# Graph attention over 32 batches: the last batch turned wholly on TensorE, with its order written out

## The reference

```python
h = jnp.maximum(_layernorm(x, axis=-1), 0.0)
q = _heads(h @ Wq + bq)
k = _heads(h @ Wk + bk)
v = _heads(h @ Wv + bv)
scores = jnp.einsum('bhqd,bhkd->bhqk', q, k) / np.sqrt(HEAD_SIZE)
bias = jnp.where(graph_mask, 0.0, NEG)[:, None]
probs = jax.nn.softmax(scores + bias, axis=-1)
ctx = jnp.einsum('bhqk,bhkd->bhqd', probs, v)
x = x + (ctx.reshape(...) @ Wf + bf)
```

## Time and profile before

| | us |
|---|---|
| median of 3 runs (676.17 to 678.21) | 677.98 |
| the profiled execution's own time | 679.02 |
| span of its trace | 677.0 |
| busy in it: PE / DVE / ACT / POOL | 628.2 / 513.2 / 506.7 / 423.5 |

### The profile page before, as it was taken

How to read it: one execution, slowest core, us unless ns; L and a number is a source line. 1 busy time by engine, 2 the same in 40 slices (tenths; PEclk the granted TensorE clock), 3 DMA queues, 4 the chain that set the end, 5 groups by cost and what they waited for, 6 DMA issues and landing times. The chain is left out here.

```text
span 677.0 us, 20551 instructions
## 1 busy us (share of the span) xinstructions
PE 628.2 (93%) x6644; PEld 510.3 (75%) x6644; DVE 513.2 (76%) x1548; ACT 506.7 (75%) x1164; POOL 423.5 (63%) x459
## 2 busy tenths in 40 slices
PE   7638899999899998999999999999999999999985
PEld 5426788888788886888778877788878888888863
DVE  5626787788788877788778887788878888887774
ACT  1435888888788886788878876788778888888872
POOL 1335666767666666776666667576666776676551
PEclk8878899999999999999999999999999999999999
DMA  7015678767787686667877676776878668767563
GB/s 241 20 34 112 127 149 159 154 149 127 160 154 160 150 162 121 150 145 158 159 145 159 153 146 120 154 160 152 159 141 155 146 141 160 160 137 134 127 136 94
DMA packets 207684, 95.89 MB, mean 142 GB/s; under 512 B 152817, under 2 KB 207602, under 8 KB 207602
## 3 DMA queue, kind: packets, MB, share of 16 engines
q1 hardware_dynamic: 207602, 94.69, 67.7%
HBM read 17.05 MB, written 12.58 MB: 44 GB/s over the span
## 5 line engine op out<-in xcount | busy, mean ns | idle before, releaser
L632 DVE CUSTOM_DVE_ANT_0 logits<-scores,mask,logit_unscale 128x256 f32<-128x256 f32 x384 | 170.6, 481 | 128.0 <-PE scores L916 124.6
L432 POOL TENSOR_TENSOR p_rows<-probs,p_rows 128x512 f16<-128x512 f32 x128 | 151.0, 1180 | 183.1 <-ACT p_rows L513 183.1
L503 ACT ACTIVATE probs<-logits,raised 128x256 f32<-128x256 f32 x384 | 174.2, 500 | 6.3
L856 PE MATMUL ring<-h_hi,w_hi 128*128 128x256 f16 x576 | 159.1, 276 | 2.6 <-DVE w_lo L723 2.6
L857 PE MATMUL ring<-h_lo,w_hi 128*128 128x256 f16 x576 | 158.8, 276 | 0.0
L858 PE MATMUL ring<-h_hi,w_lo 128*128 128x256 f16 x576 | 158.6, 275 | 0.0
L416 POOL TENSOR_TENSOR split<-qk,split 128x512 f16<-128x512 f32 x96 | 111.1, 1157 | 13.1 <-DVE split L656 13.1
L915 PE MATMUL scores<-heads 128*128 128x256 f16 x384 | 95.3, 275 | 23.0 <-DMA heads<-split 16.9
L499 ACT ACTIVATE raised<-least,p_raise 128x2 f32<-128x2 f32 x192 | 56.8, 296 | 68.4 <-DVE least L632 53.3
L525 ACT ACTIVATE qk<-ring,qk_bias_s,qkv_ratio 128x256 f32<-128x256 f32 x192 | 97.0, 555 | 9.4 <-PE ring L858 8.6
L943 PE MATMUL ctx<-v_hi,p_cols 128*128 128x65 f16 x768 | 89.5, 194 | 14.0 <-DMA p_cols<-p_rows 9.8
(11 more groups left out here) (90 smaller groups left out, 1427.2 us busy)
## 6 DMA issues: line engine op xcount, KB each, us to landing
heads<-split SPq DMA_DIRECT2D x192, 96.0 KB, 2.2
x_in<-in_x_dram SPq DMA_DIRECT2D x32, 384.0 KB, 3.4
heads<-split SPq DMA_DIRECT2D x192, 64.0 KB, 2.1
out_dram<-result SPq DMA_DIRECT2D x64, 192.0 KB, 2.1
adj_in<-in_adj_dram SPq DMA_DIRECT2D x32, 64.0 KB, 2.0
p_cols<-p_rows SPq DMA_TRANSPOSE x128, 3.1
w_raw<-in_L_gnn_Wq_dram SPq DMA_DIRECT2D x1, 576.0 KB, 4.3
w_raw<-in_L_gnn_Wk_dram SPq DMA_DIRECT2D x1, 576.0 KB, 6.3
```

The lines of the kernel that those rows point to most:

```text
L432: pool.tensor_tensor(p_rows[u][:, 1], probs[u % 3][:], p_rows[u][:, 0], ALU.subtract).then_inc(p_lo_ready, 1)
L503: act.activation(probs[u % 3][:, a], logits[u % 3][:, a], ACT.Exp, bias=raised[u % 3][:, a:a + 1], scale=-1.0).then_inc(probs_ready, 1)
L632: dve.tensor_tensor_reduce(out=logits[u % 3][:, a], in0=score_bank[u % 2][:, a * S:(a + 1) * S], in1=mask[b.parity][:, t], scale=logit_uns ...
L856: pe.matmul(out_ap, a_hi, m_hi, start=first, stop=False)
```

## The change

For batch 31 alone, and with everything up to the end of cycle 30 left as it was:

- All six units are turned on TensorE. They take turns in two banks, `pt_bank` for even units and `ring[2]` for odd ones. ACT reads the high half and DVE the low half out of the bank (`last_hi`, `last_lo`). POOL's `probs_lo` for units 1, 2, 4 and 5 and SP's four transposing DMAs of this batch fall away. The two DMA units of batch 30 that cycle 31 still has to handle stay.
- The context of batch 31's first query tile goes into `ring[3]`, that of its second into `ctx_bank`.
- PE, DVE, ACT, POOL and SP no longer run cycles 31, 32 and 33. Each has its list of steps written out. On PE `last_transpose(u)` comes two slots behind `scores(u)`.

The three helpers stand, in this order, on ScalarE, VectorE and TensorE.

```diff
+        def ctx_of(b, t):
+            bank = ring[3] if b.k == B - 1 and t == 0 else ctx_bank
+            return bank[:, 0:HEADS * V1].rearrange("p (h d) -> p h d", h=HEADS)
...
-            for k in range(FIRST_IN_LOOP + RING * TURNS, B + 2):
+            for k in range(FIRST_IN_LOOP + RING * TURNS, B - 1):
                 cycle(Batch(0, k))
+        LAST = Batch(0, B - 1)
+        last_pt = [pt_bank, ring[2]]
...
+            def last_hi(u):
+                act.wait_ge(pt_ready, nth_last(u))
+                act.activation(p_cols[u][:, 0].rearrange("p a s q -> p (a s q)"), last_pt[u % 2][:],
+                               ACT.Copy).then_inc(pt_hi_ready, 1)
...
+            exps(LAST, 1)
+            last_hi(0)
+            context_hi(LAST + -1, 0)
+            exps(LAST, 2)
+            last_hi(1)
+            exps(LAST, 3)
+            last_hi(2)
...
+            def last_lo(u):
+                dve.wait_ge(pt_hi_ready, nth_last(u))
+                dve.tensor_tensor(p_cols[u][:, 1].rearrange("p a s q -> p (a s q)"), last_pt[u % 2][:],
+                                  p_cols[u][:, 0].rearrange("p a s q -> p (a s q)"),
+                                  ALU.subtract).then_inc(pt_lo_ready, 1)
...
+            finish(LAST + -2, 1)
+            last_lo(0)
+            mask_and_max(LAST, 2)
+            context_lo(LAST + -1, 0)
+            last_lo(1)
+            mask_and_max(LAST, 3)
+            divide(LAST + -1, 1)
+            last_lo(2)
+            mask_and_max(LAST, 4)
...
+            def last_transpose(u):
+                if u == 1:
+                    pe.wait_ge(v_lo_ready, LAST.count(2, 2))
+                pe.wait_ge(pt_lo_ready, nth_last(u - 2) if u >= 2 else LAST.count(len(PE_UNITS), 0))
...
+            apply_probs(LAST, 3)
...
+            project_out(LAST + -1, 1)
+            last_transpose(5)
+            apply_probs(LAST, 4)
+            project_out(LAST, 0)
+            apply_probs(LAST, 5)
+            transpose_context(LAST, 1)
+            project_out(LAST, 1)
```

More of the change, by code:

```diff
@@ L155, in gnn_attention @@
         R_OUT = [ring[1], ring[3]]
-        ctx_ps = ctx_bank[:, 0:HEADS * V1].rearrange("p (h d) -> p h d", h=HEADS)
+        def ctx_of(b, t):
+            bank = ring[3] if b.k == B - 1 and t == 0 else ctx_bank
+            return bank[:, 0:HEADS * V1].rearrange("p (h d) -> p h d", h=HEADS)
         w_in = [sem(f"w_in{n}") for n in range(4)]
@@ L267, in cycles, with nth_last @@
                     cycle(Batch(i, FIRST_IN_LOOP + n))
-            for k in range(FIRST_IN_LOOP + RING * TURNS, B + 2):
+            for k in range(FIRST_IN_LOOP + RING * TURNS, B - 1):
                 cycle(Batch(0, k))
+        LAST = Batch(0, B - 1)
+        last_pt = [pt_bank, ring[2]]
+        def nth_last(u):
+            return (B - 1) * len(PE_UNITS) + u + 1
         def nth_dma(u):
@@ L279, in probs_read @@
         def probs_read(eng, b, u):
-            if u in PE_UNITS:
+            if b.k == B - 1:
+                eng.wait_ge(pt_ready, nth_last(u))
+            elif u in PE_UNITS:
                 wait(eng, pt_ready, b.count(len(PE_UNITS), nth_pe(u)))
@@ L386, in _ @@
             cycles(sp, cycle)
+            place_heads(LAST, 2)
+            transpose_probs(LAST + -1, 4)
+            store(LAST + -2, 0)
+            transpose_probs(LAST + -1, 5)
+            store(LAST + -2, 1)
+            for b in (LAST + -1, LAST):
+                for t in range(QT):
+                    store(b, t)
             for t in range(QT):
@@ L485, in _ @@
             cycles(pool, cycle)
+            probs_lo(LAST + -1, 5)
         @block.scalar
@@ L490, in exps @@
             def exps(b, u):
[L492 to L495, removed]
+                if u >= 3:
                     probs_read(act, b, u - 3)
+                elif (b + -1).exists():
+                    probs_read(act, b + -1, u + 3)
                 wait(act, logits_ready, b.count(2 * UNITS, 2 * u + 2))
@@ L608, in _ @@
             cycles(act, cycle)
+            def last_hi(u):
+                act.wait_ge(pt_ready, nth_last(u))
+                act.activation(p_cols[u][:, 0].rearrange("p a s q -> p (a s q)"), last_pt[u % 2][:],
+                               ACT.Copy).then_inc(pt_hi_ready, 1)
+            probs_hi(LAST + -1, 5)
+            exps(LAST, 0)
+            v_hi_part(LAST, 1)
+            exps(LAST, 1)
[5 more added lines that the diff above has]
+            last_hi(2)
+            exps(LAST, 4)
+            last_hi(3)
+            context_hi(LAST + -1, 1)
+            exps(LAST, 5)
+            last_hi(4)
+            context_hi(LAST, 0)
+            last_hi(5)
+            context_hi(LAST, 1)
         @block.vector
@@ L667, in divide @@
                 wait(dve, ctx_ready, b.count(UNITS, C * (t + 1)))
+                ctx_ps = ctx_of(b, t)
                 dve.reciprocal(inv_sum[t][:], ctx_ps[:, :, D]).then_inc(inv_ready, 1)
@@ L849, in _ @@
             cycles(dve, cycle)
+            def last_lo(u):
[3 more added lines that the diff above has]
+                                  ALU.subtract).then_inc(pt_lo_ready, 1)
+            mask_and_max(LAST, 0)
+            divide(LAST + -1, 0)
+            mask_and_max(LAST, 1)
+            v_lo_part(LAST, 1)
+            finish(LAST + -2, 1)
[7 more added lines that the diff above has]
+            mask_and_max(LAST, 4)
+            finish(LAST + -1, 0)
+            last_lo(3)
+            mask_and_max(LAST, 5)
+            divide(LAST, 0)
+            context_lo(LAST + -1, 1)
+            last_lo(4)
+            context_lo(LAST, 0)
+            finish(LAST + -1, 1)
+            last_lo(5)
+            divide(LAST, 1)
+            finish(LAST, 0)
+            context_lo(LAST, 1)
+            finish(LAST, 1)
         @block.tensor
@@ L929, in apply_probs @@
                 t, j = u // C, u % C
-                if u in PE_UNITS:
+                ctx_ps = ctx_of(b, t)
+                if b.k == B - 1:
+                    pe.wait_ge(pt_lo_ready, nth_last(u))
+                elif u in PE_UNITS:
                     wait(pe, pt_lo_ready, b.count(len(PE_UNITS), nth_pe(u)))
@@ L935, in apply_probs @@
                     wait(pe, v_lo_ready, b.count(2, 2))
-                if j == 0:
+                if u == 0 and b.k == B - 1:
+                    pe.wait_ge(result_ready, (b + -2).count(2, 2))
+                elif u == C and b.k == B - 1:
+                    pe.wait_ge(context_ready, b.count(2, 0))
+                elif j == 0:
                     wait(pe, context_ready, b.count(2, t))
@@ L1038, in _ @@
             cycles(pe, cycle)
+            def last_transpose(u):
+                if u == 1:
+                    pe.wait_ge(v_lo_ready, LAST.count(2, 2))
+                pe.wait_ge(pt_lo_ready, nth_last(u - 2) if u >= 2 else LAST.count(len(PE_UNITS), 0))
+                for a in range(2):
+                    pe.wait_ge(probs_ready, LAST.count(2 * UNITS, 2 * u + a + 1))
+                    for s in range(QT):
+                        o = (a * QT + s) * P
+                        mm = pe.transpose(last_pt[u % 2][:, o:o + P], probs[u % 3][:, a, s * P:(s + 1) * P], ident[:])
+                mm.then_inc(pt_ready, 1)
+            scores(LAST, 0)
+            apply_probs(LAST + -1, 2)
+            project_out(LAST + -2, 1)
+            scores(LAST, 1)
+            apply_probs(LAST + -1, 3)
+            last_transpose(0)
+            scores(LAST, 2)
+            transpose_context(LAST + -1, 0)
+            apply_probs(LAST + -1, 4)
+            last_transpose(1)
+            scores(LAST, 3)
+            apply_probs(LAST + -1, 5)
+            last_transpose(2)
+            apply_probs(LAST, 0)
+            scores(LAST, 4)
+            project_out(LAST + -1, 0)
+            last_transpose(3)
+            apply_probs(LAST, 1)
+            scores(LAST, 5)
+            apply_probs(LAST, 2)
+            transpose_context(LAST + -1, 1)
+            last_transpose(4)
+            apply_probs(LAST, 3)
+            transpose_context(LAST, 0)
+            project_out(LAST + -1, 1)
[5 more added lines that the diff above has]
+            project_out(LAST, 1)
 _INS = ['x', 'adj', 'L0_gnn_Wq', 'L0_gnn_bq', 'L0_gnn_Wk', 'L0_gnn_bk', 'L0_gnn_Wv', 'L0_gnn_bv',
```

## The result

| | before | changed |
|---|---|---|
| median (us) | 678.58 (10 runs, 676.17 to 682.12) | 682.04 (10 runs, 681.16 to 684.66) |
| ratio to before | | 1.0049, 95% interval 1.003 to 1.0069 |
| span of the profiled execution (us) | 677.0 | 679.6 |
| from the first logits of batch 31 to the span's end (us) | 27.05 | 31.12 |

The change makes the kernel slower by 0.49%, about 3.3 us. The forecast was 680.5 us and +0.38%. The last line of the table is the measure for all that follows: everything up to the end of cycle 30 is the same code in every kernel here, but its time differs from one execution to the next (the first logits of batch 31 stand at 649.95 us before, at 648.48 after, and between 645.96 and 651.58 in all the profiles here). I call this measure the end. The spans are given to 0.1 us, so an end is known to about 0.05 us, though it is written with two digits.

What follows compares the result with a forecast made beforehand. TensorE bounds the body, chains of waits between engines the end. Logits 4.27 us late, less 1.28 and 0.43 regained, give +2.56 us with rounding; from 677.98 the forecast is 680.5 us, range 678.8 to 682.4.

Steps and rivals of the forecast that it cites:

- What goes: Last batch, unit 5: the 5.07 us DMA way goes; by TensorE 1.65 us, so applied 3.4 us earlier if nothing else were late.
- The closed round: Last batch, units 2 to 5: DVE and ScalarE pass one unit per 3.37 us, making logits(5) 4.27 us late.
- The sum to the end: From logits(5) to the span's end: 671.71 + 7.84 = 679.55 us of span, against 677.0, or +2.56 us.
- The time: Whole kernel: 680.5 us from a median of 677.98, or +0.38%.
- The bounds of what the trace didn't show: Last batch: simultaneous bank reads cost 0 to +0.7 us, hops 0.3 us either way; ends kept at -0.3 and +1.0 us.
- The clock: Rival: TensorE, idle more at 657 to 669 us, loses clock; at most +3.3 us, 683.8 us; chance 0.07.
- The first rival: Last batch: DVE and ScalarE keep ahead, removed DMAs come through; 676.7 us, outer bound 674.6; chance 0.07.
- The Trainium skill's rule of rotating banks: Turned probabilities' two banks: filling one while the other is read would make the last batch faster; no row showed bank waits.

Runs made afterwards that it cites:

- after_again: The changed kernel unaltered, profiled a second time: 678.22 us (one run), end 29.34 us.
- e1_logits_first: Changed kernel with VectorE's logits of units 3, 4 and 5 of the last batch put ahead of low halves 1, 2 and 3: 678.93 us, ratio 0.9991.
- e3_one_bank: Changed kernel with one bank instead of two for all six turned units: 681.51 us, ratio 1.0036.
- e5_fill_all: Changed kernel with 44 extra unread matmuls in TensorE's holes, 16 of them ahead of its last two waits: 680.77 us, ratio 1.0021.
- e4_searched: Changed kernel with the last batch's same steps in an order searched for the shortest end on TensorE, VectorE and ScalarE: 673.45 us, ratio 0.9919.
- e4_again: Changed kernel with the last batch's steps in the searched order on TensorE, VectorE and ScalarE, measured once more: 673.13 us, ratio 0.9912.
- e2_fill_matmul: Changed kernel with 28 extra unread matmuls in TensorE's holes between 655 and 666 us, the last two holes left open: 681.92 us, ratio 1.0044.
- e9_dma_searched: Kernel before, units 1, 2, 4 and 5 still turned by DMA and one context bank, last batch in an order searched likewise: 675.61 us, ratio 0.9961.

## Why the prediction was right, point by point

- **What goes.** Right. No transposing DMA is in the chain, and `apply_probs(31,5)` waits for TensorE's own work. From unit 5's last probability to that step it was 5.07 us before. In after_again, where the clock held, it is 3.6 us (forecast 3.78), and `project_out(30,1)` takes the 1.47 us of the earlier trace rows (664.85 to 666.32 in its timeline).
- **The closed round.** Right, and its size to 0.02 us: 3.37 forecast, 3.35 to 3.36 measured. Unit 5's logits are 15.70 - 11.46 = 4.24 us late, forecast 4.27. e1_logits_first shows the cause: with three steps of one list swapped the loss is gone.
- **The sum to the end.** Right where no fall of the clock lies on the chain: +2.29 us (after_again), +2.35 (e3_one_bank and e5_fill_all average 29.40), against +2.56. More than half of the difference is one term: `last_transpose(5)` took 0.44 us up to TensorE's next matmul in after_again, not 0.59. One step was left out by luck without harm. In TensorE's list `transpose_context(31,0)` stands ahead of `project_out(30,1)`, and the forecast let `context_lo` of batch 30 decide instead. The chain goes through the transposes (664.38, 0.55 us), and the projection starts 17.79 us behind the first logits, where the forecast had 17.86.
- **The time.** 682.04 us is 1.54 over the forecast of 680.5. Of this 0.60 is the base: the median of the kernel before was taken from three runs as 677.98 and is 678.58 over ten. The rest is taken up under the clock. That 682.04 still lies in the range (678.8 to 682.4) is in part luck, since no term of the range stood for a clock that falls on top of the forecast.
- **The bounds of what the trace didn't show.** In the round the high half is 0.57 to 0.58 us and the low half 0.69, as before. But ScalarE and VectorE don't read there at once: VectorE idles until the high half is done. They do in e4_searched, where the high half of unit 5 (662.25, 0.59 us) overlaps with the low half of unit 4 (662.45, 0.68 us) in the other bank for 0.39 us, and neither is longer by more than 0.02 us.
- **The clock.** Here the working was wrong in part. I had it as a rival with 7 in 100, to take the place of the forecast, at most +3.3 us. It doesn't take its place but comes on top, in some executions: 1.78 us in the first profile. I reasoned that a kernel whose clock held through a hole of 2.05 us would hold it through holes of 1.3 us. The rows show that it isn't the one longest hole: with holes of 0.94, 0.77 and 0.96 us one after another it fell in the first profile (in the third of them) and held in after_again, and in e3_one_bank it fell after one of 1.89. The size was wrong too. The 1.56 came from the lengths of single matmuls in the earlier trace rows (0.42 against 0.27 us). In a chain their spacing counts, and in the same trace it is 0.21 us (19.78 to 19.99) against 0.11 (22.18 to 22.29), twice as long, as is the 0.32 against 0.16 in `project_out(30,1)`. So the bound for 5.9 us of work, were all of it spaced so, was +5.9 and not +3.3 us. The clock is the likely rest of the 3.3 us measured beyond the 2.3 of the order, but that is argued from profiles. How many executions have the fall isn't known: the mean granted clock of every run (0.975 on average over the ten of the changed kernel, against 0.977 in the profile with the fall and 0.980 in the one without) speaks for many of them. But the first slices of a run move this mean as well (e4_again's profile has 0.975 with no fall in the end), so no count follows.
- **The first rival** (the round isn't closed and the DMAs' time comes through) was wrong for this order. e1_logits_first makes its condition true for units 3 to 5: the end is 0.71 us shorter than before, where the rival had 1.3, and unit 5's logits are still 0.60 us late (12.06 against 11.46). The searched order goes beyond it: 676.7 us and at best 674.6 were the rival's numbers, and 673.1 to 673.5 came out. There the search also moved the scores forward, and unit 5's logits stand at 8.43 us.
- **The Trainium skill's rule of rotating banks** (Perfetto Trace Analysis, Matmuls) holds once the lists let it: the second bank is worth nothing in the changed kernel's order (29.40 without it, 29.34 with it) and 3.6 us in the searched one.

## What to carry to other kernels

When an order is written out, go round the waits once per unit: if engine A has step x(u-1) ahead of step y(u+1), and engine B has its part of x(u-1) behind its part of y(u), the two engines work one after the other, and each unit takes one turn of that round, whatever else is freed. Its length can be added up from a few rows of the old trace, and it came out here to two hundredths of a microsecond. While the round was closed, the faster way for a step (TensorE for the DMA) gave back 5.07 - 3.60 = 1.47 us of the 4.24 that the round cost, and the second buffer nothing. Once it was open, the second buffer was worth 3.6 us.

## What the hardware showed that I had not expected

- TensorE's granted clock at the end of one and the same program: 0.57 between 665 and 669 us in one execution, 1.00 all through the end in the next. In the kernel before, with a hole of 2.05 us, its one profile shows 1.00. The level was 0.50 of full speed where a window of 2 us lay inside such a stretch, which is 1.2 of the 2.4 GHz; in the changed kernel TensorE had worked 0.75 us between 662 and 664 us and 0.72 between 664 and 666, where the fall began, and in e3_one_bank 0.23 us between 656 and 658. With matmuls in the holes it was 1.00 up to the next hole left open (e2_fill_matmul) or to the end (e5_fill_all), one profile each; without them it did both.
- Extra matmuls in holes that are long enough cost nothing: with 44 of them the end was 29.39 us against 29.34.
- Three transposing DMAs issued 1.8 us apart took 4.7, 4.5 and 3.6 us to land (e9_dma_searched), against 3.0 to 3.1 for those issued 2.2 to 3.5 us apart in the kernel before. What else moved at the time wasn't separated.
